# Two attention steps' scores together in four PSUM tiles, the heads' sums in the tiles of the fill

## The reference

```python
# layer 0
y = einsum('nm,bmd->bnd', adj, x);  x = layernorm(x + y @ weight + bias)
# layer 1, 8 heads of 64 columns
q, k, v = split_heads(x @ w_qkv)
attn = softmax(where(adj == 0, -inf, (q @ k.T) * 64 ** -0.5))
o = (attn @ v) @ w_proj + b_proj
x = layernorm(x + o + layernorm(o) * gamma + beta)
```

## Time and profile before

| | |
|---|---|
| median of 3 runs | 3786.2 us (3785.31 to 3787.47) |
| profiled execution, first to last instruction | 3783.6 us |
| its own time beside the span | no separate time is listed; the runs' median lies 2.6 us above the span |
| busy in the span | PE 98%, PEld 76%, DVE 77%, ACT 57%, POOL 41% |
| mean granted TensorE clock | 0.991 |

### The profile page before, as it was taken

How to read it: one execution, slowest core, us unless ns; L and a number is a source line. 1 busy time by engine, 2 the same in 40 slices (tenths; PEclk the granted TensorE clock), 3 DMA queues, 4 the chain that set the end, 5 groups by cost and what they waited for, 6 DMA issues and landing times.

```text
span 3783.6 us, 64102 instructions
## 1 busy us (share of the span) xinstructions
PE 3694.9 (98%) x18960; PEld 2865.1 (76%) x18960; DVE 2911.8 (77%) x6681; ACT 2164.6 (57%) x4505; POOL 1533.9 (41%) x2311
## 2 busy tenths in 40 slices
PE   8999999989999999999999999999999999999996
PEld 6888888867777777777777777777777777777775
DVE  7666666636888888888888888888888787888887
ACT  4444444436666666666666666666666666666664
POOL 4555555522333333333333333333333333333334
PEclk9999999989999999999999999999999999999998
DMA  6555555530111111111111111111111111111111
GB/s 195 177 177 177 177 177 177 177 105 27 45 44 44 44 44 44 44 44 47 47 44 44 45 49 44 44 44 50 44 44 44 50 44 44 44 44 44 44 52 35
DMA packets 344957, 276.18 MB, mean 73 GB/s; under 512 B 13664, under 2 KB 275808, under 8 KB 344928
## 3 DMA queue, kind: packets, MB, share of 16 engines
q1 hardware_dynamic: 344928, 275.83, 24.1%
HBM read 141.56 MB, written 134.22 MB: 73 GB/s over the span
## 4 chain that ended last, share of the span: by engine, by line
PE 71%; DVE 4%; ACT 2%; issue 1%; POOL 0%; DVEq 0%; POOLq 0%
PE bank L764 20%; PE bank L778 10%; PE bank L730 10%; PE bank L796 10%; PE bank L719 9%; PE bank L745 7%; PE bank L746 6%; DVE pt_lo L931 3%; ACT pt_hi L838 1%; ACT v L849 1%; DVE probs L917 0%; DVE o_stats L957 0%; POOL probs L663 0%; DVE ot L949 0%; DVE v L942 0%
## 5 line engine op out<-in xcount | busy, mean ns | idle before, releaser
L830 ACT ACTIVATE probs<-probs,bias_row 128x512 f32<-128x512 f32 x1024 | 731.5, 716 | 441.2 <-DVE bias_row L917 441.2
L931 DVE TENSOR_TENSOR pt_lo<-bank,pt_hi 128x512 fp32r<-128x512 f32 x1024 | 694.4, 689 | 287.5 <-ACT pt_hi L838 264.7
L838 ACT ACTIVATE pt_hi<-bank 128x512 fp32r<-128x512 f32 x1024 | 556.9, 596 | 513.7 <-PE bank L730 513.7
L663 POOL TENSOR_SCALAR probs<-probs,inv_sums 128x480 f32<-128x480 f32 (+1 forms) x1024 | 687.1, 684 | 0.0
L917 DVE CUSTOM_DVE_ANT_0 probs<-bank,mask_bias 128x512 f32<-128x512 f32 x1024 | 661.5, 683 | 1.2 <-PE bank L719 1.2
L660 POOL TENSOR_TENSOR probs<-probs,inv_sums 128x32 f32<-128x32 f32 x512 | 123.3, 241 | 1155.9 <-DVE inv_sums L923 1155.6
L730 PE MATMUL bank<-ident,probs 128*128 128x128 f32 x4096 | 535.9, 274 | 15.6 <-POOL probs L663 13.7
L730 PEld LDWEIGHTS bank<-ident,probs 128*128 128x128 f32 x4096 | 480.8, 141 | 89.0 <-POOL probs L663 19.3
L669 POOL TENSOR_TENSOR o_rstd<-o_var_eps,half_neg 128x1 f32<-128x1 f32 x256 | 156.9, 613 | 725.7 <-DVE o_var_eps L962 725.7
L745 PE MATMUL bank<-pt_hi,v 128*128 128x512 f32 x1024 | 413.8, 404 | 26.6 <-DVE pt_lo L931 22.0
L764 PE MATMUL bank<-x_hi,w_hi 128*128 128x512 f32 x1024 | 411.8, 402 | 11.4 <-PEq L209 11.4
(11 more groups left out here) (90 smaller groups left out, 7654.0 us busy)
## 6 DMA issues: line engine op xcount, KB each, us to landing
x_in<-in_x_dram SPq DMA_DIRECT2D x32, 1024.0 KB, 5.6
ut_hi<-ut_hi_sb SPq DMA_DIRECT2D x128, 256.0 KB, 3.7
ut_lo<-ut_lo_sb SPq DMA_DIRECT2D x128, 256.0 KB, 3.7
u_beta_rows<-ub SPq DMA_DIRECT2D x32, 1024.0 KB, 4.4
x_hi<-ut_hi SPq DMA_DIRECT2D x128, 256.0 KB, 4.2
x_lo<-ut_lo SPq DMA_DIRECT2D x128, 256.0 KB, 4.6
out_dram<-o SPq DMA_DIRECT2D x128, 256.0 KB, 3.1
ub_row<-u_beta_rows SPq DMA_DIRECT2D x124, 256.0 KB, 2.9
```

The source lines that it names most:

```text
L663: pool.tensor_scalar(probs[:, k % 2, a, cols], probs[:, k % 2, a, cols], inv_sums[:, k % 4, a:a + 1], 0.0, ALU.mult, ALU.add)\
L830: act.activation(probs[:, k % 2, a, :], probs[:, k % 2, a, :], ACT.Exp, bias=bias_row[:, k % 4, a:a + 1], scale=-1.0, accum_out=sums[:, k ...
L838: act.activation(pt_hi[:, a, :, n * P:(n + 1) * P], t_bank[a][:].rearrange("p (m n) -> p m n", m=T), ACT.Copy)\
L931: dve.tensor_tensor(pt_lo[:, a, :, cols], t_bank[a][:].rearrange("p (m n) -> p m n", m=T), f32(pt_hi[:, a, :, cols]), ALU.subtract).then_i ...
```

## The change

1. The scores get four PSUM tiles: two for even steps and two for odd ones. PE no longer computes scores in even steps; in each odd step it computes those of steps k + 2 and k + 3, one after the other.
2. That takes two tiles more. `attend_v` now writes into the same two tiles as the fill (`o_bank = g_bank`), so it waits until the group's last two units have been read, and the fill of the next group waits for `ot_sum`.
3. `ot_halves` and `ot_sum` move to the first place in step 4, 8, 12 and 0 of the next batch (`ot_sum` was one step later).
4. The 48 fill matmuls of a group are dealt 20, 12, 16 and 0 over its parts in place of 16, 16, 16 and 0.

In the diff below the waits of `v_matmuls` and `project` are left out; they change as those of `qk_matmuls` do: the first two units of a group's fill now wait for `ot_summed`.

```diff
-            s_bank, t_bank, o_bank, g_bank = psum[0:2], psum[2:4], psum[4:6], psum[6:8]
+
+
+            s_bank, t_bank, g_bank = (psum[0:2], psum[2:4]), psum[4:6], psum[6:8]
+            o_bank = g_bank
...
+            FILL = [20, 12, 16, 0]
+            BEFORE = [sum(FILL[:n]) for n in range(T)]
...
-                            if not (isinstance(b, int) and b * STEPS + k == 0):
-                                pe.wait_ge(max_found, b * 32 + (2 * k + a - 1))
+                            if not (isinstance(b, int) and b * STEPS + k < 2):
+                                pe.wait_ge(max_found, b * 32 + (2 * k + a - 3))
...
-                                last = pe.matmul(s_bank[a][:], l[h, pair, n * P:(n + 1) * P], r[h, pair, :],
+                                last = pe.matmul(s_bank[k % 2][a][:], l[h, pair, n * P:(n + 1) * P], r[h, pair, :],
...
-                    def attend_v(b, p):
+                    def attend_v(b, p, last_part, more):
                         for a in range(2):
-
                             pe.wait_ge(ptlo_made, b * 32 + (8 * p + 7 + a))
-                            if a == 0:
-                                if p == 0:
+
+                            if p == 0:
+                                if a == 0:
                                     pe.wait_ge(vlo_made, b * 4 + 4)
-                                if not (isinstance(b, int) and b * PAIRS + p == 0):
-                                    pe.wait_ge(ot_summed, b * 8 + 2 * p)
+                            elif p == 1 and last_part:
+                                pe.wait_ge(o_made, b * 4 + (a - 1))
+                            elif p >= 2 and more:
+                                pe.wait_ge(qklo_made, b * 8 + (4 * (p - 2) + a + 11))
+                            else:
+                                pe.wait_ge(ot_summed, b * 8 + (2 * p + a - 1))
...
-                                if i >= 2:
+                                if i % 4 >= 2 or (begin and i >= 2):
                                     pe.wait_ge(qklo_made, b * 8 + (i - 1))
-                                elif not begin and isinstance(b, int) and b == 1:
-                                    pe.wait_ge(vlo_made, 3 + i)
                                 elif not begin:
-                                    pe.wait_ge(o_made, b * 4 + (i - 5))
+                                    pe.wait_ge(ot_summed, b * 8 + (i // 4 * 2 + i % 4 - 5))
...
-                            if k + 2 < STEPS or more:
-                                scores(b, k + 2)
+                            if k % 2:
+                                for ahead in (k + 2, k + 3):
+                                    if ahead < STEPS or more:
+                                        scores(b, ahead)
                             group, part = divmod(k, T)
+                            if group == 0:
+                                v_matmuls(b, BEFORE[part], FILL[part])
+                            elif group == 1 and last_part:
+                                project(b, BEFORE[part], FILL[part])
+                            elif group >= 2 and more:
+                                qk_matmuls(b + 1, 48 * (group - 2) + BEFORE[part], FILL[part])
                             if part == T - 1:
-                                attend_v(b, group)
-                            elif group == 0:
-                                v_matmuls(b, 16 * part, 16)
-                            elif group == 1 and last_part:
-                                project(b, 16 * part, 16)
-                            elif group >= 2 and more:
-                                qk_matmuls(b + 1, 48 * (group - 2) + 16 * part, 16)
+                                attend_v(b, group, last_part, more)
 
                     qk_matmuls(0, 0, 96, begin=True)
-                    scores(0, 0)
-                    scores(0, 1)
+                    for k in range(3):
...
+                            if output_at(b, k, 0) and (last_part or k >= T):
+                                ot_halves(*output_at(b, k, 0))
                             pt_hi_part(b, k)
                             if k % T == 3 and k > 3:
                                 unit_hi(b, k, 3, more)
                             if last_part and row_at(k - 2, LN_STEP) is not None:
                                 result(b, row_at(k - 2, LN_STEP))
-                            for j, stage_of in ((0, ot_halves), (2, ot_hi_part)):
-                                if output_at(b, k, j) and (last_part or k >= T):
-                                    stage_of(*output_at(b, k, j))
+                            if output_at(b, k, 2) and (last_part or k >= T):
+                                ot_hi_part(*output_at(b, k, 2))
...
+                            if output_at(b, k, 0) and (last_part or k >= T):
+                                ot_sum(*output_at(b, k, 0))
                             if k % T in (1, 2):
                                 unit_lo(b, k, k % T - 1, more)
...
-                            for j, stage_of in ((1, ot_sum), (2, ot_lo_part)):
-                                if output_at(b, k, j) and (last_part or k >= T):
-                                    stage_of(*output_at(b, k, j))
+                            if output_at(b, k, 2) and (last_part or k >= T):
+                                ot_lo_part(*output_at(b, k, 2))
```

More of the change, by code:

```diff
@@ L598, in graph_layers @@
             LN_STEP = [7, 9, 11, 13]
+            FILL = [20, 12, 16, 0]
+            BEFORE = [sum(FILL[:n]) for n in range(T)]
+            assert sum(FILL) == 48
             assert LN_STEP[-1] + 2 < STEPS
@@ L772, in v_matmuls @@
                             if g % 12 == 0:
-                                if n < 2:
-                                    pe.wait_ge(qklo_made, b * 8 + (7 + n))
+                                if n >= 2:
+                                    pe.wait_ge(vlo_made, b * 4 + (n - 1))
+                                elif isinstance(b, int) and b == 0:
+                                    pe.wait_ge(qklo_made, 7 + n)
                                 else:
-                                    pe.wait_ge(vlo_made, b * 4 + (n - 1))
+                                    pe.wait_ge(ot_summed, b * 8 + (n - 1))
                             a, c = ((xt_hi, w_hi), (xt_hi, w_lo), (xt_lo, w_hi))[s]
@@ L789, in project @@
                                 elif isinstance(b, int) and b == B:
-                                    pe.wait_ge(o_made, 4 * (B - 1) + n - 1)
+                                    pe.wait_ge(ot_summed, b * 8 + (n - 1))
                                 else:
-                                    pe.wait_ge(vlo_made, b * 4 + (3 + n))
+                                    pe.wait_ge(ot_summed, b * 8 + (n + 1))
                             if n == 0 and s == 0 and p >= PAIRS - 2:
@@ L803, in batch @@
                             turn(b, k)
-                            if k + 2 < STEPS or more:
-                                scores(b, k + 2)
+                            if k % 2:
+                                for ahead in (k + 2, k + 3):
+                                    if ahead < STEPS or more:
+                                        scores(b, ahead)
                             group, part = divmod(k, T)
-                            if part == T - 1:
-                                attend_v(b, group)
-                            elif group == 0:
-                                v_matmuls(b, 16 * part, 16)
-                            elif group == 1 and last_part:
-                                project(b, 16 * part, 16)
-                            elif group >= 2 and more:
-                                qk_matmuls(b + 1, 48 * (group - 2) + 16 * part, 16)
+                            if group == 0:
[4 more added lines that the diff above has]
+                                qk_matmuls(b + 1, 48 * (group - 2) + BEFORE[part], FILL[part])
+                            if part == T - 1:
+                                attend_v(b, group, last_part, more)
                     qk_matmuls(0, 0, 96, begin=True)
-                    scores(0, 0)
-                    scores(0, 1)
+                    for k in range(3):
+                        scores(0, k)
                     batch(0, last_part=False)
@@ L916, in masked_max @@
                         for a in range(2):
[L917 removed]
+                            dve.tensor_tensor_reduce(probs[:, k % 2, a, :], s_bank[k % 2][a][:], mask_bias[:, k % T, :],
                                                      -SCALE, 3.0e38, ALU.add, ALU.min,
```

1 line of the change is left out of this document (removed).

## The result

The changed kernel takes **3750.8 us** (median of 4 runs, 3748.5 to 3752.7) against 3786.5 for the kernel before, measured beside it. The ratio is 0.9907 with a 95% interval of 0.989 to 0.992: 35.7 us faster, where 3784 and no measurable change were forecast.

A forecast was written before the change was run, and what follows sets the result against it. PE, busy 98% of the span, was taken as the bound. Saving 4.1 us a batch against 3.95 added gave -0.15, about -5 us in 31 batches, rounded to a 2 us gain: 3786.2 becomes 3784 us, range 3768 to 3806.

The forecast's parts named there:

- The saved passages: On PE, going to 64-row matmuls and back is paid 8 times a batch instead of 16: 8 x 0.38 = 3.0 us saved.
- `attend_v`'s old waits: Products with v wait for the lo halves of their step's probabilities; a second step's scores cover this, saving 1.1 us a batch.
- sum of new waits: Four new PE waits a batch, in steps 8, 11, 15 and 3, total 3.85 us; 3.95 with the even steps' passages.
- 0.14 comes back because a pair without a wait takes 1.28 and not 1.42: DVE's `pt_lo` pairs in steps 7 and 11, entered late, regain 0.14 us of their delay.
- Step 8: PE's first fill matmul waits for `ot_summed` from DVE: 1.0 to 1.3 us, taken as 1.15.
- Step 3: PE's first head of `attend_v` waits for v_lo and `pt_lo`: 0.2 to 0.55 us, taken as 0.4.
- Step 11: PE's second head of `attend_v` waits for DVE's k_lo: 1.75 to 2.1 us, taken as 1.9.
- Step 15: PE's second head waits for k_lo, without a layer norm on DVE: 0.25 to 0.65 us, taken as 0.4.
- The first: Rival, faster: the new waits are at their lower ends, 3.2 us, net -0.9 a batch, 3758 us; chance 0.25.
- The second: Rival, slower: passages from transposes to full matmuls cost 0.10 each, 0.8 us a batch, 3806 us; chance 0.12.
- The third: Rival, much slower: step 11's wait drops PE's clock to 1.2 GHz, about 4 us more a batch, 3900 us; chance 0.03.
- The signs that the prediction named for being wrong: The four waits sum to under 3.2 or over 4.6 us, or step 0, 4 or 12 waits as well.

The follow-up runs named there:

- experiment 1: The changed kernel with each step making its own scores again, on the same four tiles, and one wait for the masks' reads: 3900.6 us, ratio to before 1.030.
- Experiment 4: The changed kernel with DVE's second `pt_lo` in part 2 of each group waiting for a fill unit, about when scores used to end: 3770.4 us, ratio 0.996.
- experiment 5: The changed kernel with the first row's layer norm moved on DVE from the end of step 7 to behind step 8's `ot_sum`: 3767.9 us, ratio 0.995.

## Why the prediction was wrong

**The saved passages were right.** Eight a batch at 0.38 were forecast; the part lengths are met within 0.01 us, and experiment 1 shows the price from the other side (8 x 0.39 come back with the scores of every step). The Trainium skill has a rule for this (TensorEngine Tiling (Array Packing), section "Key Properties"): a change of tiling mode drains TensorE. The rows agree, with 0.11 us more between matmuls at each change and a slower first one, and none between transposes and full matmuls.

**The end of `attend_v`'s old waits was right** to 0.1: steps 3, 7, 11 and 15 of before stand 0.49, 0.23, 0.13 and 0.15 above 5.63, together 1.0 for 1.1. Its fill steps are 5.69 and not 5.68, and in all 4.2 is saved for 4.1.

**The step that failed** is in the sum of new waits: "0.14 comes back because a pair without a wait takes 1.28 and not 1.42". It took the 0.14 in the earlier trace rows for a consequence of waiting for ACT, and credited it in steps 7 and 11 only, where DVE enters late. The 0.14 is the second `pt_lo`'s wait for the scores of its own step, which end 1.93 after the transposes (2005.22 + 0.40 against 2003.69). The pair of the earlier trace rows is short because it starts too late to meet them. For step 10 the sum even charged the 0.14 again (6.15 - 0.76 + 0.14 = 5.53): once `ot_sum` no longer delays that pair, it was to take 1.42. Two pairs in the changed kernel, of steps 9 and 10, show which wait it is. Both stand idle for ACT first; only step 9, in which PE makes scores, has the long pair:

```profile
1958.67 1.43 DVE L945 TENSOR_TENSOR pt_lo<-bank,pt_hi 128x512 fp32r<-128x512 f32 x2 [0.67 <-ACT pt_hi L851]
...
1964.13 1.29 DVE L945 TENSOR_TENSOR pt_lo<-bank,pt_hi 128x512 fp32r<-128x512 f32 x2 [0.44 <-ACT pt_hi L851]
```

The change takes the scores out of even steps, so the pair is short in steps 2, 6, 10 and 14 too, and DVE enters the step behind each of them about 0.14 earlier. Behind each of the four stands one of the four waits. Experiment 4 puts the old arrival back and makes each of the four waits longer by 0.14 to 0.16, 0.59 a batch, and with it 3770 us. The diff and the order of DVE's rows named both semaphores of the second `pt_lo`; no sum followed that second one.

**The four waits, one by one.** Step 8: 0.90 for 1.15; 0.14 is the arrival, and 0.1 or more was my choice within 1.0 to 1.3, where the working itself gave 8.2 - 7.20 = 1.0. Step 3: 0.15 for 0.4; 0.16 is the arrival, and the other 0.1 my choice within 0.2 to 0.55. In steps 3 and 8 no price of starting anew is added: the first matmul behind the wait (0.49 and 0.50 long, the next 0.33 and 0.34 behind it) follows scores or transposes, where without a wait the next comes 0.34 and 0.32 behind it as well. Step 11: 1.89 for 1.9, a hit by two misses: idle time is 0.15 to 0.2 shorter than forecast, the restart adds 0.11, and the row-by-row sum had 1.93. Step 15: 0.37 for 0.4, again a hit by two misses: k_lo starts 4.00 after the transposes and not 4.15, which takes 0.15 off, and the restart adds 0.11. The forecast's total was 0.54 a batch too high, 17 us in 31 batches, and this alone moves 3784 to 3767, just below the lower end of the range.

**The other half of the miss.** A batch is 0.87 shorter where 0.15 was forecast. Of these 0.72, 0.54 are the waits, 0.1 the larger saving, and 0.08 the charge of 0.01 for each passage of the even steps, which the step lengths don't show; 22 us in 30 batches. Rounding the gain of 5 us down to 2 took 3 more. And 8 us came outside the 30 batches, where almost nothing was forecast. Together these are the 33 us between 3784 and 3750.8. The 8 can be traced in part. 1.3 lie in the first stage, which the change doesn't touch: the second stage's first matmul stands at 791.58 and at 792.84 before, and between 791.2 and 793.4 in all the kernels here. 1.7 are the start of the second stage: before, the scores of step 1 waited 1.83 for `masked_max` to free their tile, and DVE's reciprocal for step 0 stands behind the mask of step 1; with four tiles they don't wait. 2.1 are step 0 of the first batch (5.82 for 7.92; 0.16 of it is the usual saving). Before, PE stands idle for 1.83 and then 2.45 ahead of it, and over 824 to 832 the granted clock is 0.70; with the change it stands idle for 1.13 and 1.21, and over 821 to 827 the clock is 1.00:

```profile
824.00 1.97 PE L730 MATMUL bank<-ident,probs 128*128 128x128 f32 x8 [2.45 <-POOL probs L663]
```

```profile
821.04 1.33 PE L737 MATMUL bank<-ident,probs 128*128 128x128 f32 x8 [1.21 <-POOL probs L670]
```

The remaining 1.9 of the first batch are the usual saving with few waits, as DVE has no layer norm of a batch before: step 8 is 5.54, steps 11 and 15 are 6.65 each. The forecast gave this batch the same -0.15 as the others. In the last batch 2.7 was gained, likewise without the fill's waits, and 1.3 lost behind it; no run parts these further.

**The rivals.** The first had nearly the right batch (-0.9 for -0.87) for a cause of the wrong kind: not waits that happened to fall to their lower ends (3.2; the waits of steps 3 and 8 are below theirs, those of steps 11 and 15 above), but one arrival that four of them share. The second is refuted by the 0.79 in the rows above: parts 0 are 5.54 and would be 5.63 with 0.10 a passage. The third did not happen in the changed kernel: step 11 took 8.21 to 8.23 in all 30 full batches. But its mechanism stood close by. Moving one layer norm (experiment 5) made that wait 0.3 longer, and the clock fell in 21 of 30 batches. The Trainium skill (TensorE: Matmul & The Clock Gate, section "HAM oscillation — how this bites in real kernels") says that an engine that idles between bursts of work drops to its lower clock; experiments 1 and 5 agree for 8 and for 21 of their 30 batches, with 0.43 between matmuls in place of 0.23.

**What the sum could not hold.** The forecast was a difference of two numbers near 4 us, each made of several DVE terms known to 0.1 or 0.2. An error of 0.14 four times is 0.46% of the time, over twice what a measurement can tell. The range of 38 us allowed for each wait's bounds, but a common error moves all four together; with that in mind the "faster" side deserved more than 0.25. The signs that the prediction named for being wrong did not show: the four waits sum to 3.3, inside its 3.2 to 4.6, and steps 0, 4 and 12 wait for nothing. A total of the waits that leaves 43 us of room in 31 batches is too coarse a sign for a forecast within 0.2%.

## What to carry to other kernels

When a change moves an instruction, list every semaphore that counts it and look at who waits there, even where today's trace shows no named wait: a gap hidden in an x2 group, seen only as 1.42 in place of 1.28, was a wait on the moved scores, and it set how long four others last. When tiles get shared between two producers, the row that frees a tile is at the path's head, so look for work ahead of it on the helper engine: moving k_lo ahead of the mask and the layer norm gave 68 us, nearly twice what the change itself gave. And remove waits from the longest down, since shortening an early one can push a later one further, here into a wait after which the clock falls.

## What the hardware showed

- TensorE's clock fell to 1.2 GHz after idle times of 1.87 or 1.88 us in 21 of 30 batches of experiment 5 and of 2.01 or 2.02 in 8 of 30 of experiment 1 (granted clock 0.84 and 0.83 over 10 us around one of each). It did not in the 30 full batches of experiment 4 (idle 1.72 to 1.80) or of the changed kernel (1.58 to 1.60), nor after 2.00 in the last batch of the kernel before. The length of a wait alone doesn't decide: within experiment 5 eight batches with the same 1.87 or 1.88 kept the clock, and within experiment 1 all 22 others with 2.01 to 2.08. Nor does the order of work ahead of the wait, which is the same in every one of these batches. What does decide is open.
- A matmul that starts after a wait in the middle of full matmuls (the second heads of steps 11 and 15) takes 0.50 us and the next comes 0.34 or 0.33 behind it: about 0.11 more than the pace of 0.23. Where it follows a change of mode or transposes, the same 0.32 to 0.34 stands there without a wait, and the wait adds nothing to it. The view of waits, which counts idle time from the end of the matmul before (0.39 long, where the next could have started 0.23 behind it), shows 1.58 for a wait that lengthens its step by 1.89.
